# Experts' down projection in three fp32r passes, behind the next expert's gate and up

## The reference

```
x = x + 0.5 * ffn(layernorm(x));  x = x + attention(layernorm(x));  x = x + 0.5 * ffn(layernorm(x))

ffn(h):  z = w_norm * rms_norm(h);  probs = softmax(z @ w_router)        # 32 experts
         each token takes its 4 best experts; each expert takes at most 128 tokens
         y_e = (silu(z_e @ w_gate[e]) * (z_e @ w_up[e])) @ w_down[e]     # 256 -> 176 -> 256
         out = sum of probs * y_e over a token's experts
             + sigmoid(z @ w_shared_gate) * ((silu(z @ sw_gate) * (z @ sw_up)) @ sw_down)   # 256 -> 704 -> 256
         return h + out
```

## Time and profile before

| | us |
|---|---|
| median of 3 runs (lowest, highest) | 937.8 (937.79, 938.08) |
| the profiled execution | 938.85 |
| its span | 937.0 |
| PE busy | 909.6 (97%) |
| DVE busy | 695.9 (74%) |
| ACT busy | 531.3 (57%) |
| GpSimd busy | 511.1 (55%) |

### The profile page before, as it was taken

The page is one execution under the profiler, slowest core; times in us unless marked ns, Lnnn a source line. Parts: engine busy times, 40 slices in busy tenths (PEclk is TensorE's granted clock), DMA queues, the critical chain, the costliest instruction groups (busy, mean ns, idle before and its releaser), DMA issues.

```text
span 937.0 us, 18000 instructions
## 1 busy us (share of the span) xinstructions
PE 909.6 (97%) x6118; PEld 685.6 (73%) x6118; DVE 695.9 (74%) x1704; ACT 531.3 (57%) x794; POOL 511.1 (55%) x537
## 2 busy tenths in 40 slices
PE   7999999999999999999999999989999999999997
PEld 6878887777778856666666666558788878777786
DVE  6998787555355889989998999988887875544435
ACT  6666743132233478878887888876667531322322
POOL 6343305565553588887888788934432055555530
PEclk9999999999999999999999999999999999999999
DMA  7143247777783610011001002004432377777735
GB/s 260 46 138 109 74 131 183 172 178 174 185 199 59 202 47 24 23 35 32 23 23 41 26 12 79 24 12 131 142 99 73 97 203 173 175 182 177 173 35 178
DMA packets 95512, 101.89 MB, mean 109 GB/s; under 512 B 18768, under 2 KB 86736, under 8 KB 95440
## 3 DMA queue, kind: packets, MB, share of 16 engines
q1 hardware_dynamic: 83152, 83.17, 29.5%
q0 software_dynamic: 12288, 17.83, 11.2%
HBM read 65.44 MB, written 35.54 MB: 108 GB/s over the span
## 4 chain that ended last, share of the span: by engine, by line
PE 63%; DVE 18%; issue 9%; ACT 4%; POOL 4%; DMA 1%; DVEq 0%; POOLq 0%; ACTq 0%
PE zT L1050 7%; PE gu L90 6%; PE gu L92 6%; PE gu L91 6%; PE gu L1070 6%; PE pj_at L90 3%; PE pv_at L1765 3%; PE pj_at L92 3%; PE pj_at L91 3%; PE down L90 3%; PE down L92 3%; PE down L91 3%; PE scores_at L1749 2%; PE zT L1059 2%; DVE turned_at L2007 2%
## 5 line engine op out<-in xcount | busy, mean ns | idle before, releaser
L90 PE MATMUL gu<-x_hi,gu_hi 128*128 128x512 f32 x264 | 120.4, 456 | 0.8 <-DVE act_gu L1353 0.7
L825 POOL DMA_INDIRECT rows<-z_rows,slots x64 | 69.3, 1083 | 67.9 <-DVE slots L1344 48.9
L1867 ACT ACTIVATE capped_at<-scores_at 128x2048 f32<-128x2048 f32 x64 | 93.1, 1454 | 20.5 <-PE scores_at L1749 20.3
L1130 ACT CAST a_hi<-act_gu 128x512 fp32r<-128x512 f32 x96 | 59.2, 617 | 79.1 <-DVE act_gu L1353 65.9
L92 PE MATMUL gu<-x_lo,gu_hi 128*128 128x512 f32 x264 | 103.9, 393 | 0.0
L91 PE MATMUL gu<-x_hi,gu_lo 128*128 128x512 f32 x264 | 103.6, 393 | 0.0
L1875 ACT ACTIVATE probs_at<-capped_at 128x2048 f32<-128x2048 f32 x64 | 95.1, 1487 | 2.5
L90 PE MATMUL down<-down_hi,a_hi 128*128 128x256 f32 x300 | 93.9, 313 | 0.6 <-DVE a_lo L1363 0.4
L1944 POOL TENSOR_SCALAR_AFFINE_SELECT probs_at<-probs_at 128x1024 f32<-128x1024 f32 x64 | 85.5, 1340 | 9.7 <-ACT probs_at L1875 9.0
L1050 PE MATMUL zT<-w_gu,xT 128*128 128x352 f32 x256 | 86.3, 460 | 0.0
L1232 ACT ACTIVATE y<-gu,rows 128x256 f32<-128x256 f32 x64 | 30.3, 473 | 98.5 <-PE gu L1070 89.0
(11 more groups left out here) (262 smaller groups left out, 2603.3 us busy)
## 6 DMA issues: line engine op xcount, KB each, us to landing
w_gu<-in_w_gate SPq DMA_DIRECT2D x64, 176.0 KB, 2.7
w_gu<-in_w_up SPq DMA_DIRECT2D x64, 176.0 KB, 3.3
w_down<-in_w_down SPq DMA_DIRECT2D x64, 176.0 KB
z_rows<-z SPq DMA_DIRECT2D x16, 512.0 KB, 3.6
acc<-base SPq DMA_DIRECT2D x10, 512.0 KB, 3.4
out<-base SPq DMA_DIRECT2D x10, 512.0 KB, 3.3
xn_at<-acc SPq DMA_DIRECT2D x16, 256.0 KB, 2.8
x<-xn_at SPq DMA_DIRECT2D x16, 256.0 KB, 2.1
```

The source lines that it names most:

```text
L90: nc.tensor.matmul(out, w_hi, x_hi, start=first, stop=False)
L825: pool.indirect_dma_start(out=gathered_rows[:, n, :], out_offset=None, in_=m.z_rows, in_offset=bass.IndirectOffsetOnAxis(ap=slots[:, e:e + ...
L1867: nc.scalar.activation(capped[:, u % 2, :, 0:n], scores[:, :, 0:n], ACT.Tanh, scale=QK_SCALE / SOFTCAP).then_inc(capped_ready, 1)
```

## The change

The down projection of an expert is computed like the shared expert's, from high and low parts. ACT casts the high part of the transposed products (`high_products`) and of the down weights (`high_down`), DVE subtracts for the low parts (`low_products`, `low_down`). Raw down weights are held for 3 experts, their parts for 2. The y buffers move into the memory of block 7's base, and the transposed products into the other half of y's PSUM bank, so that `turn_products` waits until the result of the expert before is scaled.

The down projection of e-1 moves behind gate and up of e and the row transposes of e+1; that of expert 0 stands ahead of gate and up of expert 1, that of expert 31 behind the first piece after the loop. ACT's and DVE's queues are put in an order to match. List building moves to e = 1, 3, ..., 11, in two halves. SP's later loads wait for `weights_due`, which a memset of one word on GpSimd raises behind the issue of add e-4 and ahead of a gather.

```diff
-            for e in range(HELD_W):
-                if e == EARLY - 1:
-                    reached(sp, gathered[1], 16)
-                if e >= EARLY:
-                    load_gate_up(e)
-                load_down(e)
+            load_down(0)
+            load_down(1)
+            reached(sp, gathered[1], 16)
+            load_down(2)
+            load_gate_up(EARLY)
             for e in range(HELD_W, E):
+                reached(sp, weights_due, e - HELD_W + 1)
+                load_down(e - 1)
                 reached(sp, gu_done, e - HELD_W + 1)
                 load_gate_up(e)
-                reached(sp, y_ready, e - HELD_W + 1)
-                load_down(e)
+            load_down(E - 1)
...
             for e in range(E):
                 add(e)
+                if e + HELD_W < E:
+                    pool.memset(tick[:, e:e + 1], 0.0).then_inc(weights_due, 1)
                 if e + HELD_ROWS < E:
                     gather(e + HELD_ROWS)
...
             def turn_products(e):
                 reached(pe, prod_done, e + 1)
-                reached(pe, xT_copied, min(e + 2, E))
...
                 at_least(pe, y_scaled, e)
...
+            def down_expert(e):
+                n = e % 2
+                reached(pe, w_down_lo_made, e + 1)
+                reached(pe, prodT_lo_ready, e + 1)
+                for k in range(2):
+                    last = split_matmul(nc, y_ps, prodT_hi[:, k, :], prodT_lo[:, k, :], w_down_hi[:, n, k, :],
+                                        w_down_lo[:, n, k, :], k == 0, k == 1)
                 last.then_inc(y_ready, 1)
...
             for e in range(E):
+                if e == 1:
+                    down_expert(0)
+                gate_up_expert(e)
                 if e + 1 < E:
                     turn_rows(e + 1)
-                gate_up_expert(e)
-                *earlier_pieces, last_piece = pieces_beside(e)
-                for p in earlier_pieces:
+                if e > 1:
+                    down_expert(e - 1)
+                first_piece, *later_pieces = pieces_beside(e)
+                piece(first_piece)
+                turn_products(e)
+                for p in later_pieces:
                     piece(p)
-                turn_products(e)
-                piece(last_piece)
                 if e < 12 and e % 2 == 0:
                     find(2 + e // 2)
-                down_expert(e)
...
+            def high_products(e):
+                reached(act, prodT_ready, e + 1)
+                at_least(act, y_ready, e)
+                nc.scalar.copy(prodT_hi[:], prodT_ps).then_inc(prodT_hi_ready, 1)
+
+            def high_down(e):
+                reached(act, w_down_loaded[e % HELD_D], 16 * (e // HELD_D + 1))
+                at_least(act, y_ready, e - 1)
+                nc.scalar.copy(w_down_hi[:, e % 2], w_down[:, e % HELD_D]).then_inc(w_down_hi_made, 1)
...
             for e in range(E):
+                if e == 1:
+                    scale(0)
                 silu_expert(e)
-                for p in pieces_beside(e):
+                if e > 1:
+                    scale(e - 1)
+                first_piece, *later_pieces = pieces_beside(e)
+                followup(first_piece)
+                high_products(e)
+                for p in later_pieces:
                     followup(p)
-                scale(e)
+                high_down(e)
...
+            def low_products(e):
+                reached(dve, prodT_hi_ready, e + 1)
+                dve.tensor_tensor(prodT_lo[:], prodT_ps, prodT_hi[:].bitcast(F32), ALU.subtract).then_inc(prodT_lo_ready, 1)
+
+            def low_down(e):
+                reached(dve, w_down_hi_made, e + 1)
+                dve.tensor_tensor(w_down_lo[:, e % 2], w_down[:, e % HELD_D], w_down_hi[:, e % 2].bitcast(F32), ALU.subtract
+                                  ).then_inc(w_down_lo_made, 1)
...
             for e in range(E):
+                lists = e < 12 and e % 2 == 1
+                if e > 0:
+                    low_down(e - 1)
+                product_expert(e)
                 if e + 1 < E:
                     copy_rows(e + 1)
-                first, *middle, last_piece = pieces_beside(e)
-                followup(first)
-                product_expert(e)
-                for p in middle:
+                if lists:
+                    list_places(2 + e // 2)
+                first_piece, *later_pieces = pieces_beside(e)
+                followup(first_piece)
+                low_products(e)
+                if lists:
+                    list_tokens(2 + e // 2)
+                for p in later_pieces:
                     followup(p)
-                copy_products(e)
-                followup(last_piece)
-                if e < 12 and e % 2 == 0:
-                    list_experts(2 + e // 2)
+            low_down(E - 1)
```

More of the change, by code:

```diff
@@ L50 @@
 HELD_W = 4
+HELD_D = 3
 HELD_ROWS = 6
@@ L475, in ffn @@
         in_tile = sb("in_tile", [P, E8, P], BF16)
-        to_end = sb("to_end", [P, E8, P], BF16)
         below = sb("below", [P, 2, 4, P - 1], BF16)
-        xT = sb("xT", [P, 2, KC, CAP], F32)
+        with ExitStack() as until_listed:
+            to_end = sb("to_end", [P, E8, P], BF16, until_listed)
         silu_e = sb("silu_e", [P, 2, FE], F32)
         prod = sb("prod", [P, 2, FE], F32)
-        prodT = sb("prodT", [FD, 2, 2, CAP], F32)
-        y = sb("y", [P, HELD_Y, C], F32)
-        w_down = sb("w_down", [FD, HELD_W, 2, C], F32)
+        xT = sb("xT", [P, 2, KC, CAP], F32)
+        prodT_hi = sb("prodT_hi", [FD, 2, CAP], F32R)
+        prodT_lo = sb("prodT_lo", [FD, 2, CAP], F32R)
+        w_down = sb("w_down", [FD, HELD_D, 2, C], F32)
+        w_down_hi = sb("w_down_hi", [FD, 2, 2, C], F32R)
+        w_down_lo = sb("w_down_lo", [FD, 2, 2, C], F32R)
         if attention_next:
@@ L494, in ffn @@
         warm = sb("warm", [P, 1], F32)
+        tick = sb("tick", [1, E], F32)
         logitsT = sb("logitsT", [P, BLK], F32)
@@ L518, in ffn @@
         x_lo = [x_lo[:, n] for n in range(HELD_X - 1)] + [x_lo_third[:], x_lo_fourth[:]]
+        y = base[:, HELD_X - 1]
         base = [base[:, n] for n in range(HELD_X)] + [base_fourth[:]]
@@ L569, in ffn @@
         w_gu_loaded = [sem(f"w_gu_loaded{n}", 32 * (E // HELD_W)) for n in range(HELD_W)]
-        w_down_loaded = [sem(f"w_down_loaded{n}", 16 * (E // HELD_W)) for n in range(HELD_W)]
+        w_down_loaded = [sem(f"w_down_loaded{n}", 16 * len(range(n, E, HELD_D))) for n in range(HELD_D)]
+        w_down_hi_made = sem("w_down_hi_made", E)
+        w_down_lo_made = sem("w_down_lo_made", E)
         gathered = [sem(f"gathered{n}", 16 * len(range(n, E, HELD_ROWS))) for n in range(HELD_ROWS)]
@@ L577, in ffn @@
         prodT_ready = sem("prodT_ready", E)
-        prodT_copied = sem("prodT_copied", E)
+        prodT_hi_ready = sem("prodT_hi_ready", E)
+        prodT_lo_ready = sem("prodT_lo_ready", E)
         y_ready = sem("y_ready", E)
@@ L581, in ffn @@
         added = sem("added", 16 * E)
+        weights_due = sem("weights_due", E - HELD_W)
         def block_rows(dram, b):
@@ L738, in load_down @@
             def load_down(e):
-                sp.dma_start(w_down[:, e % HELD_W, :, :], ins["w_down"][e].rearrange("(p k) n -> p k n", k=2)
-                             ).then_inc(w_down_loaded[e % HELD_W], 16)
+                at_least(sp, w_down_lo_made, e - HELD_D + 1)
+                sp.dma_start(w_down[:, e % HELD_D, :, :], ins["w_down"][e].rearrange("(p k) n -> p k n", k=2)
+                             ).then_inc(w_down_loaded[e % HELD_D], 16)
             def slot(b, f, r, s):
@@ L1056, in turn_products @@
                 reached(pe, prod_done, e + 1)
-                reached(pe, xT_copied, min(e + 2, E))
+                if e == 0:
+                    reached(pe, lists_ready, 2)
+                at_least(pe, y_scaled, e)
                 for k in range(2):
@@ L1062, in down_expert @@
             def down_expert(e):
[L1063 to L1068, removed]
+                n = e % 2
+                reached(pe, w_down_lo_made, e + 1)
+                reached(pe, prodT_lo_ready, e + 1)
                 for k in range(2):
-                    last = nc.tensor.matmul(y_ps, prodT[:, e % 2, k, :], w_down[:, n, k, :], start=k == 0, stop=k == 1)
+                    last = split_matmul(nc, y_ps, prodT_hi[:, k, :], prodT_lo[:, k, :], w_down_hi[:, n, k, :],
+                                        w_down_lo[:, n, k, :], k == 0, k == 1)
                 last.then_inc(y_ready, 1)
@@ L1339, in list_experts, with list_tokens @@
                                                ALU.mult), done + 1)
+            def list_tokens(r):
+                s = r % 2
+                done = 3 + 2 * r
                 with nc.allow_low_precision(reason="counts up to 127"):
@@ L1345, in list_experts @@
                                          in1=local[:, s], op0=ALU.add, op1=ALU.add).then_inc(lists_ready, 1)
+            def list_experts(r):
+                list_places(r)
```

(1 more changed line is left out.)

15 lines of the change are left out of this document (8 added, 7 removed).

## The result

The changed kernel takes 967.4 us (median; 966.15 to 971.07) against 937.8 before: ratio 1.0315, 95% interval 1.0300 to 1.0329. The forecast was 950.0 with a range of 927 to 959: the sign and the mechanism came, the size was 17.4 us short. The profiled execution is the longest of these, 971.07 us (span 969.3).

A forecast was written before the change was run, and what follows sets the result against it. PE's expert loop was taken as the bound: -8.0 - 5.7 + 1.0 + 19.3 = +6.6 us per stage, +5.3 in the first, together +11.9 on the profiled 938.85; less 1.05 to the median, 949.7, forecast 950, range 927 to 959.

The forecast's parts named there:

- Stalls on the weight split: Seam between expert iterations: PE's down projection waits for ACT's weight cast and DVE's subtraction, +19.3 us per stage.
- the walk: Queues of PE, ACT and DVE followed in written order through the expert loop; stalls by iteration, together 19.3 us.
- What PE saves: Expert loop on PE: down projection 0.70 us instead of 0.95, 8.0 us saved per stage.
- The scaling as the next wait: Product transposes wait for the scaling of the expert before: 0.03 us lost per expert, 1 us per stage.
- rival 4: Product transposes wait on scaling, so PE's 0.25 us per expert are lost; 8 us per stage more, 966 us, chance 0.03.
- The wait for the products: Expert loop: PE's wait before the product transposes goes, some 0.18 us per expert, 5.7 us per stage.
- Adds and weights: Word on GpSimd, reordered requests and moved loads in the expert loop cost nothing; cover some 5 us.
- First stage: Attention's rows land before PE needs them, so 1.3 us of loss goes: +5.3 us for this stage.
- Rival 1: Seam between iterations: splits hide, PE's loop falls by up to 12.7 us per stage, adds then bound; 922 us, chance 0.22.

The follow-up runs named there:

- two kernels: Changed kernel with requests by the rule of before and no word: 966.3 us; kernel before with the word and later requests waiting for it: 939.0 us.
- the kernel with the cast alone earlier: Changed kernel with ACT's weight cast right behind the cast of the products, DVE's weight subtraction left first in the next iteration; 948.6 us, 1.0104 of before.
- the kernel with the gaps filled less: Changed kernel with 8, 10, 6 and 10 filler matmuls in its four longest gaps per stage (a first filling had 15, 10, 6, 10); 965.5 us.

## Why the prediction was right or wrong

- **Stalls on the weight split: right.** By iteration, gaps in the first loop of 2.3, 1.8, 1.2 (1 to 3), 0.2, 0.7 (6, 8), 1.2, 0.9 (10, 11), 0.7, 0.8, 1.5, 0.4, 0.3 (13, 14, 16, 17, 19), 1.4, 0.7, 0.8, 1.2, 1.8 (23, 25, 26, 28, 30): the 17 iterations of the walk, 17.9 for its 19.3. Behind each gap the first matmul takes 0.1 more, 1.7 in all, which the walk did not have.
- **What PE saves: this step failed.** I priced the down projection by 0.95 from start to start, in an old neighbourhood, against six fp32r matmuls in a run of their kind. At one and the same place the difference is 0.15, so 4.8 us per stage and not 8.0: 3.2 too much.
- **The scaling as the next wait: seen, mis-sized.** PE goes on 0.15 after ACT's end, where I took 0.05, a little less than the 0.06 that the earlier trace rows show from DVE to PE. 0.12 per expert instead of 0.03: 3.9 us per stage by the starts, 2.9 too little. This is rival 4's mechanism at about a third of its price. That its 966 lies beside the measured time is chance.
- **The wait for the products** went, as said. **Adds and weights**: right, by two kernels; the word is 0.55 us, past my bound of 0.31, and still hidden. **First stage**: the second loop starts at 771.73 at full clock, 13.2 later, with the first loop 14.1 longer: 0.9 gained in between where 1.3 was said.
- **Weight subtraction beside GpSimd: no term in the sum, and PE shows none.** All 32 weight subtractions of the first loop take 0.68 to 0.69 us. In the pair of the earlier trace rows the add starts first, at 190.92, and the subtraction, at 191.96, inside it; neither is longer than the others, 1.59 and 0.69 us. In the other order the gather took longer: here one gather starts inside a weight subtraction and takes 1.43 us, the next doesn't and takes 1.05.

```profile
181.21 0.68 DVE L1593 TENSOR_TENSOR w_down_lo<-w_down,w_down_hi 88x512 fp32r<-88x512 f32 x1
181.38 1.43 POOL L836 DMA_INDIRECT rows<-z_rows,slots  x1 [0.27 <-DVE slots L1386]
...
186.11 1.05 POOL L836 DMA_INDIRECT rows<-z_rows,slots  x1 [0.27 <-issue]
```

Of the 60 gathers from 147 us on, 19 start inside such a subtraction (L1593, or L1409 of the shared expert, each 0.68 to 0.69 long), and they take 1.04 to 1.49 us: 1.05 with 0.11 of the subtraction left, 1.22 with 0.30, 1.43 with 0.51, 1.49 with 0.62. The others take 1.00 to 1.07, but for one of 1.20. The kernel before has such gathers too (1.43 at 206.79). What the 19 take over 1.05 each sums to some 3 us of GpSimd's queue over both stages, and no wait of PE in the loops names it.
- **The clock: missing.** No term and no rival had PE's clock in it, though the forecast itself made gaps of 2.5 us. 2.0 in the median.

The sum: at full clock a loop takes 160.0 us (147.16 to 307.13), 14.1 more than before, of which 0.7 is the piece that now stands inside. 13.4 against +6.6 is 6.8 too little; 3.2 + 2.9 + 1.7 - 1.4 = 6.4 of it has a name, 0.4 per stage has none. Twice 6.8, 0.4 for the first stage, 2.0 for the clock and the 1.05 by which the profiled execution of before stood over its median make 17.1 of the 17.4.

Rival 1's mechanism was real and its price was not: with no wait for the weight split left, the kernel is level with before. The saving at PE was 4.8 of the 8.0 that I gave it, the wait for the scaling takes 3.9, and waits for other work of ACT and DVE take 5.9.

## What to carry to other kernels

An instruction that only prepares later data (a cast, a split) belongs in its queue ahead of work whose input comes late, not behind it; nothing else was changed for 24 us. Price a replaced operation at the place where it will stand and next to what will stand there: a start-to-start distance holds a part that belongs to its neighbours (0.08 of the 0.95 here). Where a forecast contains gaps on TensorE of a microsecond or two, it needs a term for the clock behind them (here 0.50 for 3 to 7 us behind four gaps, 2.0 us in the median), and a hand-over price for each pair of engines (0.15 from ACT to PE, 0.06 from DVE to PE).

## What the hardware showed that I had not expected

- In the changed kernel's first stage TensorE's clock fell to 0.50 behind waits of 2.26 and 1.61 us (ended at 152.91 and 299.74) of an engine busy until then (for the first, 9.9 of the 10 us from 140 on), and its falls in both stages lasted 3 to 7 us each; behind a wait of 1.63 us that ended at 162.26 it did not. In the kernel with the cast alone earlier it stayed at 1.00 behind a wait of 2.20 us (ended at 152.90), so the length of the wait alone doesn't tell. Matmuls that compute nothing of use, put into the gaps, held it at 0.999 over the span (the kernel with the gaps filled less).
- ACT's end to PE's start took 0.15 us (234.32 to 234.47), DVE's end to PE's start 0.06 (232.78 to 232.84).
- A memset of one word on GpSimd took 0.55 us, half as long as the instruction that issues a 128-row gather (1.1).
- A gather's issue on GpSimd took up to 1.49 us instead of 1.05 when it started inside one of DVE's subtractions for a low part (L1593, L1409), while the subtraction kept its 0.69.
